# A bottleneck layer with per-sequence experts: down 0 split around tile 1's transposition, a new order in the head, and the last tile's gT_lo behind tile 31's final pass

## The reference

```python
# x: 64 sequences x 64 rows x 512, itok: the expert (1 or 2; E = 3) of each sequence
Wd, bd, Wu, bu, g, b = W_down[itok], b_down[itok], W_up[itok], b_up[itok], ln_w[itok], ln_b[itok]
h = einsum('bsh,bhk->bsk', x, Wd) + bd          # 512 -> 256
h = gelu(h, exact)
h = einsum('bsk,bkh->bsh', h, Wu) + bu          # 256 -> 512
h = x + h
mean, var = h.mean(-1), ((h - mean) ** 2).mean(-1)
out = (h - mean) * rsqrt(var + 1e-5) * g + b
```

## Time and profile before

| what | value |
|---|---|
| time, median of 3 runs | 137.83 us (137.77 to 138.47) |
| the profiled execution | 137.71 us, span 135.9 us, granted TensorE clock 0.988 |
| TensorE busy (products) | 126.1 us, 93% of the span |
| DVE busy | 113.3 us, 83% |
| POOL busy | 104.6 us, 77% |
| ACT busy | 84.9 us, 62% |

### The profile page before, as it was taken

One profiled execution on the slowest core, in us unless ns is written; L12 is line 12 of the kernel. 1 busy time (PEld: TensorE's weight loads), 2 busy tenths in 40 slices (PEclk: granted clock), 3 DMA queues, 4 the chain that ended last, 5 costly groups with the idle time before them and its releaser, 6 DMA issues.

```text
span 135.9 us, 4056 instructions
## 1 busy us (share of the span) xinstructions
PE 126.1 (93%) x846; PEld 112.7 (83%) x847; DVE 113.3 (83%) x276; ACT 84.9 (62%) x179; POOL 104.6 (77%) x118
## 2 busy tenths in 40 slices
PE   6995989999999999999999999999999999999830
PEld 6884967999999997999999999999999999998610
DVE  1797699889879997888888898888788978897992
ACT  0766686647665778667666666666666666666600
POOL 7001984568989998889888888888888889889960
PEclk9999999999999999999999999999999999999995
DMA  1968777996554564455545445455556633331366
GB/s 35 341 205 269 236 239 257 263 253 188 164 180 140 151 171 127 144 157 150 161 150 154 154 157 154 154 154 154 154 154 161 148 77 80 77 77 42 82 166 178
DMA packets 13249, 21.95 MB, mean 161 GB/s; under 512 B 2345, under 2 KB 3890, under 8 KB 13234
## 3 DMA queue, kind: packets, MB, share of 16 engines
q1 hardware_dynamic: 8850, 15.74, 40.3%
q10 hardware_dynamic: 4384, 6.05, 15.5%
HBM read 13.39 MB, written 8.65 MB: 162 GB/s over the span
## 4 chain that ended last, share of the span: by engine, by line
PE 55%; POOL 11%; SPq 10%; DMA 7%; issue 6%; DVE 4%; POOLq 3%; ACT 2%; ACTq 1%; DVEq 0%
PE hg_ps L887 21%; PE y_ps L921 21%; POOL res L402 8%; DMA lnb_rows<-in_L_cond_ln_b_dram 7%; PE xT_ps L873 6%; SPq L249 5%; PE xT_ps L832 3%; PE hg_ps L896 3%; POOL xb L385 2%; POOLq L215 2%; SPq L255 2%; DVE res L748 1%; SPq L281 1%; ACT normed L499 1%; POOL rstd L391 1%
## 5 line engine op out<-in xcount | busy, mean ns | idle before, releaser
L385 POOL TENSOR_TENSOR xb<-x_sb,bu_rows 128x512 f32<-128x512 f32 x33 | 42.8, 1299 | 10.1 <-DVE bu_rows L687 9.8
L402 POOL TENSOR_TENSOR res<-normed,lnb_rows 128x512 f32<-128x512 f32 x31 | 39.7, 1282 | 8.7 <-ACT normed L499 8.1
L479 ACT ACTIVATE g<-hb 128x256 f32<-128x256 f32 x33 | 13.8, 419 | 35.4 <-DVE hb L700 35.4
L712 DVE BATCH_NORM_STATS2 r_stats<-y_ps 128x6 f32<-128x512 f32 x33 | 22.9, 694 | 5.8 <-issue 5.8
L921 PE MATMUL y_ps<-wu_hi,gT_hi 128*128 (+1 forms) x66 | 23.3, 433 | 1.2 <-ACT gT_hi L484 1.2
L692 DVE TENSOR_TENSOR xT_lo<-xT_ps,xT_hi 128x512 fp32r<-128x512 f32 x33 | 22.7, 687 | 1.7 <-ACT xT_hi L474 1.7
L887 PE MATMUL hg_ps<-wd_hi,xT_hi 128*128 x132 | 23.9, 303 | 0.0
L733 DVE SCALAR_TENSOR_TENSOR scaled<-y_ps,r_mv,lnw_rows 128x512 f32<-128x512 f32 x31 | 23.0, 744 | 0.4 <-issue 0.2
L391 POOL TENSOR_TENSOR rstd<-var_eps,half_neg 128x1 f32<-128x1 f32 x33 | 18.1, 549 | 6.3 <-DVE var_eps L721 5.9
L499 ACT ACTIVATE normed<-scaled,rstd 128x512 f32<-128x512 f32 x31 | 22.3, 722 | 0.0
L873 PE MATMUL xT_ps<-ident,x_sb 128*128 128x128 f32 x132 | 19.7, 273 | 1.6 <-DMA x_sb<-in_x_dram 1.6
(11 more groups left out here) (88 smaller groups left out, 150.1 us busy)
## 6 DMA issues: line engine op xcount, KB each, us to landing
x_sb<-in_x_dram SPq DMA_DIRECT2D x64, 128.0 KB, 2.8
out_dram<-res ACTq DMA_DIRECT2D x33, 128.0 KB, 2.4
out_dram<-res SPq DMA_DIRECT2D x33, 128.0 KB, 2.4
wd<-in_L_cond_W_down_dram ACTq DMA_DIRECT2D x3, 512.0 KB, 4.9
wu<-in_L_cond_W_up_dram SPq DMA_DIRECT2D x6, 256.0 KB, 3.7
lnw_rows<-in_L_cond_ln_w_dram SPq DMA_DIRECT2D x1, 768.0 KB, 8.3
lnb_rows<-in_L_cond_ln_b_dram SPq DMA_DIRECT2D x1, 768.0 KB, 9.9
x_sb<-in_x_dram ACTq DMA_DIRECT2D x2, 128.0 KB, 3.3
```

Of the source, the lines that this page charges most:

```text
L385: pool.tensor_tensor(xb[:, c % DEEP, :], x_sb[:, c % FAR, :], bu_rows[:, ds(e * H, H)], ALU.add).then_inc(xb_ready, 1)
L402: pool.tensor_tensor(res[:, c % FAR, :], normed[:, c % DEEP, :], lnb_rows[:, ds(e * H, H)], ALU.add).then_inc(res_ready, 1)
L712: dve.bn_stats(r_stats[:, c % DEEP, :], y_ps[c % YBANKS][:]).then_inc(stats_ready, 1)
```

## The change

Six edits, all of order:

- TensorE: `down(0)` is cut in two. Its eight xT_hi products stand ahead of `transpose_x(1)`, the four xT_lo products behind it. `down(2)` stands ahead of `transpose_g(1)`. `up(1)` takes its gT_lo pair ahead of its wu_lo pair.
- ACT, head: `keep_down_bias(1)` ahead of `x_hi(1)`; the two casts of each up weight are apart, with `gelu`, `x_hi` or `g_hi` between them; `seed(1)` ahead of `gelu(1)`, `x_hi(4)` ahead of `gelu(3)`.
- ACT, tile 10: one `rescale` ahead of `gelu(10)`, `g_hi(10)` ahead of the other; tile 11 is written out, and the loop begins at tile 12. The three register loads for the last stores are spread over the tiles 28 to 30.
- DVE, head: `down_bias(0)` ahead of `x_lo(1)`, `down_bias(1)` behind the second part of wu_lo, part 3 behind `g_lo(1)`.
- SP: tile 5's rows ahead of ln_w. In both queues tile 31 is stored ahead of tile 30.
- DVE, tail: `g_lo(32)` behind `scale_last(31)` and `shift_last(31)`.

```diff
 @block.sync
             load_w_up(sp, 2, slot_expert(2, head_regs[2]))
+            load(5, 5, entries(5, 0, 2))
             sp.dma_start(lnw_rows[:], rows_of(ln_w, P)).then_inc(lnw_in, 16)
-            for t in range(5, 7):
-                load(t, t, entries(t, 0, 2))
+            load(6, 6, entries(6, 0, 2))
             sp.dma_start(lnb_rows[:], rows_of(ln_b, P)).then_inc(lnb_in, 16)
...
-            for i in range(EARLY):
+            for i in (1, 0, 2):
                 t = TILES - EARLY + i
 @block.scalar
-            def wu_high(slot):
-                for k in range(KB):
...
+            def wu_high(slot, k):
...
             x_hi(0, 0)
             keep_down_bias(0)
+            keep_down_bias(1)
             x_hi(1, 1)
-            keep_down_bias(1)
+            wu_high(0, 0)
             gelu(0, 0)
-            wu_high(0)
+            wu_high(0, 1)
             g_hi(0, 0)
             x_hi(2, 2)
+            seed(1, 1)
+            wu_high(1, 0)
             gelu(1, 1)
-            seed(1, 1)
-            wu_high(1)
+            wu_high(1, 1)
             g_hi(1, 1)
             x_hi(3, 3)
             gelu(2, 2)
-            wu_high(2)
+            wu_high(2, 0)
             g_hi(2, 2)
+            wu_high(2, 1)
             seed(2, 2)
-
+            x_hi(4, 4)
             gelu(3, 3)
-            x_hi(4, 4)
             seed(3, 3)
...
+                if t == LATE:
+                    rescale(t - 4, t - 4)
                 gelu(t, t)
...
                 seed(t, t)
-                rescale(t - 4, t - 4)
+                if t < LATE:
+                    rescale(t - 4, t - 4)
+            g_hi(LATE, LATE)
             rescale(LATE - 3, LATE - 3)
+            seed(LATE + 1, LATE + 1)
+            store(LATE + 1 - STORE_B_LAG, LATE + 1 - STORE_B_LAG)
+            gelu(LATE + 1, LATE + 1)
+            x_hi(LATE + 3, LATE + 3)
+            rescale(LATE - 2, LATE - 2)
...
-            tiles(act, body, LATE + 1, TILES - 3)
+            tiles(act, body, LATE + 2, TILES - 3)
...
-            for t, batch in zip(range(TILES - EARLY, TILES), last_places):
-                store(t, t, batch)
+            for t in (last - 3, last - 1, last - 2, last):
+                store(t, t, last_places[t])
 @block.vector
             x_lo(0, 0)
-            x_lo(1, 1)
             dve.wait_ge(bd_ready, len(bd_banks))
             down_bias(0, 0, first_experts[0])
+            x_lo(1, 1)
...
             w_up_low(dve, 0, 0).then_inc(wu_lo_ready, 1)
-            down_bias(1, 1, first_experts[1])
             g_lo(0, 0)
             w_up_low(dve, 0, 1).then_inc(wu_lo_ready, 1)
+            down_bias(1, 1, first_experts[1])
             x_lo(2, 2)
             w_up_low(dve, 1, 0).then_inc(wu_lo_ready, 1)
-            w_up_low(dve, 1, 1).then_inc(wu_lo_ready, 1)
             down_bias(2, 2, first_experts[2])
             g_lo(1, 1)
+            w_up_low(dve, 1, 1).then_inc(wu_lo_ready, 1)
             x_lo(3, 3)
...
             variance(last - 1, last - 1)
-            g_lo(last, last)
             scale_last(last - 1, e_last[1])
             shift_last(last - 1, e_last[1])
+            g_lo(last, last)
             stats(last, last)
 @block.tensor
+            def down(t, c, e, halves=(xT_hi, xT_lo)):
...
+                    if x_half not in halves:
+                        continue
...
-                mm.then_inc(h_ready, 1)
+                if xT_lo in halves:
+                    mm.then_inc(h_ready, 1)
...
-                if isinstance(t, int) and t in (0, E - 1):
+                if isinstance(t, int) and t < E:
                     parts = ((gT_hi, wu_hi), (gT_lo, wu_hi), (gT_hi, wu_lo))
...
             transpose_x(0, 0)
+            pe.wait_ge(wd_hi_ready, E)
+            down(0, 0, e_first, (xT_hi,))
             transpose_x(1, 1)
-            pe.wait_ge(wd_hi_ready, E)
-            down(0, 0, e_first)
+            down(0, 0, e_first, (xT_lo,))
...
+            down(2, 2, e_down)
             transpose_g(1, 1)
-            down(2, 2, e_down)
             transpose_x(3, 3)
             up(1, 1, e_up)
```

More of the change, by code:

```diff
@@ L500, in rescale @@
                                scale=rstd[:, c % DEEP:c % DEEP + 1]).then_inc(normed_ready, 1)
-            def wu_high(slot):
-                for k in range(KB):
-                    act.wait_ge(wu_in[slot * KB + k], 16)
-                    act.copy(wu_hi[:, (slot * KB + k) * H:(slot * KB + k + 1) * H], wu[:, slot, k, :]).then_inc(
-                        wu_hi_ready, 1)
+            def wu_high(slot, k):
+                act.wait_ge(wu_in[slot * KB + k], 16)
+                act.copy(wu_hi[:, (slot * KB + k) * H:(slot * KB + k + 1) * H], wu[:, slot, k, :]).then_inc(
+                    wu_hi_ready, 1)
             def wd_high(e):
@@ L569, in _ @@
                 seed(t, t)
-                rescale(t - 4, t - 4)
+                if t < LATE:
+                    rescale(t - 4, t - 4)
+            g_hi(LATE, LATE)
             rescale(LATE - 3, LATE - 3)
+            seed(LATE + 1, LATE + 1)
[3 more added lines that the diff above has]
+            rescale(LATE - 2, LATE - 2)
+            last_places = {}
             def body(t, c):
@@ L580, in body @@
                 rescale(t - 3, c - 3)
-            tiles(act, body, LATE + 1, TILES - 3)
-            last_places = [place(t) for t in range(TILES - EARLY, TILES)]
+                if isinstance(t, int):
+                    for n in (t + 1, t + 2) if t == TILES - EARLY - 2 else (t + 2,):
+                        last_places[n] = place(n)
+            tiles(act, body, LATE + 2, TILES - 3)
             last = TILES - 1
@@ L599, in _ @@
             store(last - 4, last - 4)
-            store(last - 3, last - 3)
-            for t, batch in zip(range(TILES - EARLY, TILES), last_places):
-                store(t, t, batch)
+            for t in (last - 3, last - 1, last - 2, last):
+                store(t, t, last_places[t])
         @block.vector
@@ L874, in transpose_x @@
                 mm.then_inc(xT_ready, 1)
-            def down(t, c, e):
+            def down(t, c, e, halves=(xT_hi, xT_lo)):
                 w0 = e * (KH * BN)
```

## The result

The changed kernel takes 136.97 us (median of 6, 136.93 to 137.40) against 137.86 us (6, 137.66 to 138.47): a ratio of 0.9942 with an interval of 0.9928 to 0.9957. That is 0.9 us faster by the medians and 0.8 by the ratio. The forecast was 138.1, slower by 0.3. A second comparison of the same two gave 0.9933 (0.9909 to 0.9956). In the runs that follow, four executions (251.83 us in e1, 139.64 and 139.96 in e8, 138.90 in e10) were in a slower state: the ratios leave them out, the medians and ranges hold them.

The account below looks back on a forecast made before the run. The prediction took TensorE's unbroken work as the bound, with DVE setting the end. Head -0.15, middle -0.55 and tail +1.0 gave +0.3 on 137.71, or 138.0, plus 0.12 for the median: 138.1 us, range 137.1 to 138.8.

Parts of the forecast that it names:

- The tail, +1.0: At the end, tile 32's gT_lo behind tile 31's passes makes tile 32's statistics 1.0 us later: 1.0 lost.
- the sign that I had named for being right: In the tail, DVE idle for 0.8 to 1.0 us between tile 32's gT_lo and its statistics.
- The stores, 0: At the end, stores only change places and register loads lie in ACT's idle time: no term in the sum.
- Rival C: Tail costs nothing, as tile 32's statistics wait for something else in both kernels: -0.7, 137.1 us; chance 0.12.
- The middle, -0.55: At tiles 10 and 11, moving an ACT rescale ahead of gelu 10 removes TensorE's one stop: 0.55 us won.
- The head, -0.15: In the head, down 0 starts before tile 1's rows; of TensorE's gain, 0.15 us was taken as won.
- wu_lo part 0 over 1 us: Head, sign for being right: wu_lo part 0 on DVE, held by GpSimd, takes more than 1 us.
- The 0.39 us of issue behind it stays: Head, behind up 1's last pair: TensorE's stop at 22.98, which the profile calls issue, remains 0.39 us.
- What I had as 0.2 there: Head: up 1 starts at 21.0, 0.2 us after TensorE could, behind ACT's gT_hi.
- Rival B: Head loses 0.3 us by tile 2's late wu_lo cast; sign: transposition of g 3 after 26.3; 138.6 us; chance 0.12.
- ln_w, 0: Issued behind tile 5's rows, ln_w lands by 28.5 at worst, not needed before: cost 0, at worst 0.3 us.

Follow-up runs that it names:

- e1: The kernel before with only tile 32's gT_lo moved behind both passes of tile 31: 137.84 us against 137.99, ratio 0.9991.
- e8: The changed kernel with eight small products between the second and third pair of tile 32's up, to keep TensorE awake: 138.41 us, ratio 1.0026 to before.
- e10: The changed kernel, tile 32's gT_lo back, half the stores of tiles 27 and 28 on SP, GpSimd's third xb late: 136.61 us against 137.88 before.
- e2: The kernel before with only tile 31 stored ahead of tile 30 and the last stores' register loads read earlier: 137.33 us against 137.99.
- e5: The changed kernel with tile 32's gT_lo put back ahead of both passes of tile 31: 136.73 us against 137.99 before.
- e3: The kernel before with only ACT's new order at tiles 10 and 11: 137.21 us against 137.99, ratio 0.9932.
- e4: The changed kernel with the head of the kernel before: 137.14 us against 138.05 before, ratio 0.9934.
- the second set: The changed kernel again, e4, e6 and e8 beside new runs of the kernel before (138.05 us); the changed kernel took 137.18, difference -0.87.
- the square above: Stores' edit and moved gT_lo: neither (e3, -0.78 us), stores only (e5, -1.26), gT_lo only (e6, -0.73), both (changed kernel, -0.87).
- e9: The changed kernel with GpSimd's third xb moved behind the six small steps that follow it: 136.91 us against 137.88 before.
- the changed kernel again: The changed kernel unaltered, run a second time: 137.18 us against 138.05 before, ratio 0.9933.
- e6: The changed kernel with the old order of the last stores and register loads: 137.32 us against 138.05 before, ratio 0.9929.

## Why the prediction was wrong, step by step

**The tail, +1.0, failed.** The step was: "Tile 31's store starts 0.3 earlier, but it isn't the one that ends last." It was: it landed at 135.4, 1.5 behind tile 32's skipped store. The cost inside was right (statistics 1.00 later; the lone pair, DVE's wait of 1.31 or 0.82), and so the sign that I had named for being right, DVE idle for 0.8 to 1.0 us ahead of them, did show while the time did not move. But I followed only the engines' rows to the last instruction and never asked what the last instruction waited for. Three things were there to be read in the trace of before: SP's 1.4 us of waits for stores at its last line, tile 31's issue at 132.74, 1.8 behind its result, and a store of tile 32 that took 0.15 us. From them the slack of tile 32's chain could be worked out: SP's 1.4 us. Once the chain is 1.0 later it still ends 0.3 to 0.4 under the landing, and e1's profile has that 0.3. e1 shows the price alone, -0.15 (within 0.3 either way).

**The stores, 0, failed.** The step was: "the stores change places only with each other, and the register loads that lay between are in ACT's idle time." One of them, tile 29's, lay in the queue between stores, in front of the one store that ended the kernel. Worth 0.66 alone (e2) and 0.48 behind the middle (e5 against e3).

**Rival C** ("the tail costs nothing", 137.1) came out within 0.15 of the time, which lies just below the stated range (137.1 to 138.8), but for another reason than it gave: the statistics did wait, and what hid it lay outside all five engines. It got 0.12, because I weighed it against TensorE and DVE alone.

**The middle, -0.55, was right** in place and mechanism; 0.56 in the pair of profiles, 0.78 in the medians (0.6 to 1.3), since the old stop ranges from 0.52 to 1.03. One step of it was off without cost: gelu 10 came at 50.93 and not at 50.35, yet gT_hi of tile 10 ended at 52.6, ahead of need.

**The head, -0.15, measured 0** in the times (with it 0.04 and 0.05 slower in the two pairs, within the noise) and +0.11 in the pair of profiles. The last pairs of up 0 and up 1 held within 0.14 (18.17 for 18.31, 22.10 for 22.1; wu_lo part 0 over 1 us, 1.19), but not the products ahead of them: down 0 began at 12.10, not 11.85, so its eight products were not inside the wait for tile 1, whose transposition moved to 13.07 from 12.84, and down 1 began at 14.63, not 14.2. The sentence "The 0.39 us of issue behind it stays" failed: the stop became 0.58 at 22.98. And up 1 began at 21.08 behind a new stop of 0.34, as ACT's gT_hi of tile 1 now follows its transposition with nothing of TensorE's between but four transpositions. What I had as 0.2 there was 0.34. Rival B's sign, the transposition of g 3 later than 26.3, showed as well (26.48), but the 0.3 that went with it did not.

**ln_w, 0, was right**: issued at 20.06, it took 6.1 us (8.3 in the earlier trace rows) and landed at 26.2, well ahead of the 28.5 allowed.

The account, for the profiled pair: -0.46 upstream of the tail and -0.31 in all (137.71 to 137.40). The +0.15 between them is what is left over where the end passes from a landing to tile 32's chain. With the pair at the full clock that chain ends 0.49 sooner, which gives 136.9, and the five other executions are there. That the clock is what parts them is read from one profile against five times, was not tried by itself, and e4's profiled execution, with the low clock at its median time, does not bear it out. In the medians, in place of the forecast's -0.15 for the head, -0.55 for the middle, 0 for the stores and +1.0 for the tail, stand 0, -0.78, -0.48 and +0.39, which is the -0.87 of the second set: the end is what the forecast had wrong.

## What to carry to other kernels

Read the last wait of the program first, ahead of any engine's tail: if it is a landing, the end is set by when the last full store is issued, and the queue ahead of it (here five stores 0.66 to 1.27 us apart, the widest gap with a register load in it) is the place to look. A move that makes one of two chains near the end later has to be priced by the slack to the other, and not by its own length; take both edits apart and together, as in the square above. And where one engine's gap closes in a head, subtract the next engine's gate from it before counting: here two orders reached the same point at 22.98 in both profiles of the first pair. Last, name signs that hang on the end of the program too: here the signs for being right showed in the engines' rows, and the forecast was wrong all the same.

## What the hardware showed that was not expected

- A lone pair of 512-column products behind 1.33 to 1.35 us of idle time took 0.73 us at 2.4 GHz in three profiles (e1, e9, the changed kernel again) and 1.21 to 1.22 us at 1.2 GHz in two others (the changed kernel, e4), with 0.78 in a sixth (e6), whose clock fell within it: the same program may or may not pay 0.5 us there.
- A store that is skipped costs its queue 0.15 to 0.17 us, against 0.47 to 0.51 of most full ones, and the program's last line does not wait for a landing of it.
- A full store of 64 rows landed 2.3 to 3.0 us behind its issue among the last ones of the kernels before and after: the kernel's median of 2.4 is not the number to place the last landing with.
- Eight float32 products of 128 columns stand in e8's trace as 16 TensorE instructions, 1.95 us in all, 0.12 each.
